# A twelve-stage transformer block on one core: LayerNorm's tiles shared by VectorE and ScalarE, small products in step with its statistics, one barrier per stage, gathers issued further ahead, and the last sums made in the output

## The reference

```
def _layernorm(x, axis=-1, eps=1e-05):
    m = jnp.mean(x, axis=axis, keepdims=True)
    v = jnp.var(x, axis=axis, keepdims=True)
    return (x - m) / jnp.sqrt(v + eps)
...
    x = x + _L0_xattn_ref(_layernorm(x, axis=-1), ctx_768, ...)   # 16 heads of 64 over the context
    x = x + _L0_attn_ref(_layernorm(x, axis=-1), ...)             # 16 heads of 16, relative bias
    x = x + _L0_ffn_ref(_layernorm(x, axis=-1), ...)              # gated, FP4 quantised
    x = x + _L1_xattn_ref(_layernorm(x, axis=-1), ctx_768, ...)
    x = x + _L1_attn_ref(_layernorm(x, axis=-1), ...)             # one head of 256
    x = x + _L1_ffn_ref(_layernorm(x, axis=-1), ...)              # low rank
    x = x + _L2_xattn_ref(_layernorm(x, axis=-1), ctx_768, ...)
    x = x + _L2_attn_ref(_layernorm(x, axis=-1), ...)             # a scan over the 32 tokens
    x = x + _L2_ffn_ref(_layernorm(x, axis=-1), ...)              # 8 experts, top 2, capacity 160
    x = x + _L3_xattn_ref(_layernorm(x, axis=-1), ctx_768, ...)
    x = x + _L3_attn_ref(_layernorm(x, axis=-1), ...)
    x = x + _L3_ffn_ref(_layernorm(x, axis=-1), ...)              # 8 experts, top 2, gelu
    return x
```

## Time and profile before

| what | value |
| --- | --- |
| median of 3 runs | 1863.27 us (1859.93 to 1864.88) |
| the profiled execution, its own time | 1854.92 us |
| its span, first to last instruction | 1852.8 us |
| mean granted TensorE clock | 0.939 of full speed |
| PE busy | 1617.7 us, 87% |
| DVE busy | 1109.5 us, 60% |
| ACT busy, POOL busy | 817.1 us, 792.2 us |

### The profile page before, as it was taken

How to read it: one execution, slowest core, us unless ns; L and a number is a source line. 1 busy time by engine, 2 the same in 40 slices (tenths; PEclk the granted TensorE clock), 3 DMA queues, 4 the chain that set the end, 5 groups by cost and what they waited for, 6 DMA issues and landing times. The chain is left out here.

```text
span 1852.8 us, 35956 instructions
## 1 busy us (share of the span) xinstructions
PE 1617.7 (87%) x12777; PEld 1376.1 (74%) x12777; DVE 1109.5 (60%) x3057; ACT 817.1 (44%) x2383; POOL 792.2 (43%) x934
## 2 busy tenths in 40 slices
PE   6999999766887999987899999969959888859997
PEld 5899989634556999965798889845648745548996
DVE  5888786468854888845666766728951132363331
ACT  4766666213324888831666666620003212113332
POOL 7656656253337999833111111116732420102332
PEclk9999999789897999998999999989969989979998
DMA  8554554200013343302533333251036285761222
GB/s 257 176 169 152 175 164 153 79 1 1 1 28 121 137 139 124 130 18 90 162 107 113 115 106 114 82 187 36 1 103 205 30 210 138 253 218 36 37 40 46
DMA packets 139520, 206.20 MB, mean 111 GB/s; under 512 B 21410, under 2 KB 107106, under 8 KB 138706
## 3 DMA queue, kind: packets, MB, share of 16 engines
q1 hardware_dynamic: 131922, 194.07, 32.8%
q0 software_dynamic: 6720, 8.79, 3.0%
q10 hardware_dynamic: 704, 1.05, 0.2%
HBM read 163.53 MB, written 42.19 MB: 111 GB/s over the span
## 5 line engine op out<-in xcount | busy, mean ns | idle before, releaser
L810 DVE TENSOR_SCALAR xattn_oT<-bank,xattn_last 128x256 f32<-128x256 f32 x256 | 111.8, 478 | 91.7 <-PE bank L631 91.7
L716 ACT ACTIVATE xattn_probs<-bank,xattn_negmax 128x257 f32<-128x257 f32 x256 | 123.7, 483 | 65.5 <-DVE xattn_negmax L791 65.4
L721 ACT ACTIVATE xattn_probs<-xattn_probs,xattn_rsum 128x257 f32<-128x257 f32 x256 | 131.9, 515 | 1.4 <-DVE xattn_rsum L795 1.4
L1036 POOL TENSOR_SCALAR xattn_probs<-xattn_probs,xattn_rsum 128x257 f32<-128x257 f32 x128 | 119.5, 933 | 23.6 <-DVE xattn_rsum L1273 23.5
L791 DVE TENSOR_REDUCE xattn_negmax<-bank 128x1 f32<-128x257 f32 x256 | 106.5, 416 | 34.8 <-PE bank L604 33.2
L800 DVE TENSOR_TENSOR xattn_probsT_lo<-bank,xattn_probsT_hi 128x256 fp32r<-128x256 f32 x256 | 105.1, 410 | 9.8 <-ACT xattn_probsT_hi L727 8.7
L611 PE MATMUL bank<-ident,xattn_probs 128*128 128x128 f32 x512 | 103.9, 285 | 7.0 <-ACT xattn_probs L721 6.5
L147 ACT COPY xnT<-bank 128x512 f32<-128x512 f32 x40 | 21.4, 590 | 200.6 <-PE bank L137 200.6
L727 ACT CAST xattn_probsT_hi<-bank 128x256 fp32r<-128x256 f32 x256 | 95.4, 373 | 32.3 <-PE bank L611 28.2
L549 POOL COPY ctx_stat<-xattn_mv 128x2 f32<-128x2 f32 x32 | 6.0, 188 | 237.9 <-DVE xattn_mv L824 237.9
L600 PE MATMUL bank<-xattn_ctxT,xattn_qk_hi 128*128 128x258 f32 x256 | 93.8, 367 | 0.5 <-DVE xattn_qk L787 0.5
(11 more groups left out here) (488 smaller groups left out, 5332.6 us busy)
## 6 DMA issues: line engine op xcount, KB each, us to landing
xattn_ctxT<-ctx_partsT SPq DMA_DIRECT2D x64, 516.0 KB, 4.0
xattn_ctxN<-ctx_partsN SPq DMA_DIRECT2D x64, 384.0 KB, 4.2
ctx_partsT<-xattn_ctxT SPq DMA_DIRECT2D x32, 516.0 KB, 2.6
moe_w<-in_L_ffn_W SPq DMA_DIRECT2D x16, 1024.0 KB, 12.9
ctx_partsN<-xattn_ctxN SPq DMA_DIRECT2D x32, 384.0 KB, 3.5
moecap_w_early<-in_L_ffn_w SPq DMA_DIRECT2D x10, 1024.0 KB, 9.3
xattn_rawN<-in_ctx SPq DMA_DIRECT2D x32, 192.0 KB, 2.7
xattn_raw<-in_ctx SPq DMA_DIRECT2D x32, 192.0 KB, 4.3
```

What stands on the lines that cost most here:

```text
L716: nc.scalar.activation(probs[:, n % RING, :], SB[n % 2][:, 0:KV], ACT.Exp, bias=negmax[:, n % RING:n % RING + 1], accum_out=psum[:, n % RI ...
L721: nc.scalar.mul(probs[:, n % RING, :], probs[:, n % RING, :], rsum[:, n % RING:n % RING + 1]).then_inc(norm_ready, 1)
L810: nc.vector.tensor_scalar(oT[k][:, heads, b, :], by_head(OB[:, k * 2 * P:(k + 1) * 2 * P]), last[:, k, j * PER_TILE + b:j * PER_TILE + b + ...
L1036: nc.gpsimd.tensor_scalar(probs[:, n % RING, :], probs[:, n % RING, :], rsum[:, n % RING:n % RING + 1], None, ALU.mult).then_inc(norm_read ...
```

## The change

- **One barrier.** `Stage.end` has no barrier of its own. The semaphores of a stage are cleared by POOL once the Block's barrier is passed, while the other engines are already in the next stage, and their numbers are kept from use for one stage (`resting`).
- **Shared LayerNorm.** With `shared=True` the tiles 2, 3, 6 and 7 are normalised by ACT as x times rstd plus shift. DVE computes shift, minus mean times rstd, for two tiles at once. This holds in nine stages (xattn0, attn0, attn1, lowrank, xattn2, scan, moecap, attn3, moe). ACT does its four tiles ahead of its first copy of xnT.
- **Warm products.** `warm` issues two of the bf16 products after each tile's statistics, 16 in all, ahead of the transposes. It stands in xattn0, attn0, xattn2, scan, moecap and moe, where there was nothing, and takes the place of keep_busy in attn1, attn3 and xattn3. lowrank keeps its 34.
- **Gathers.** In moecap XS + 1 experts are gathered ahead, and then each gather goes one expert further.
- **Sums in the output.** moe's table of sums is the output tensor itself, with 128 spare rows that the host cuts off. The eight copies are gone. SP waits for the last additions.

```
@@ Stage.end
-        self.core.nc.clear_and_free_semaphores(self.sems)
-        self.core.nc.all_engine_barrier()
+        core, nc = self.core, self.core.nc
+        nc.clear_and_free_semaphores(self.sems)
+        for rested in core.resting:
+            nc.release_semaphore(rested)
+        core.resting = [nc.alloc_semaphore(f"{self.name}_rests{k}", num=sem.num) for k, sem in enumerate(self.sems)]
@@ Norm
+        self.by_act = [t for t in range(TILES) if shared and t % 4 >= 2]
+        self.by_dve = [t for t in range(TILES) if t not in self.by_act]
...
             dve.wait_ge(self.rstd_ready, h + 1)
+            theirs = [t for t in half if t in self.by_act]
+            if theirs:
+                of = slice(theirs[0], theirs[-1] + 1)
+                nc.vector.scalar_tensor_tensor(self.shift[:, of], self.mv[:, of, 0], -1.0, self.rstd[:, of],
+                                               ALU.mult, ALU.mult).then_inc(self.shift_ready, 1)
             for t in half:
-                nc.vector.tensor_scalar(xn[:, t, :], x[:, t, :], self.mv[:, t, 0:1], self.rstd[:, t:t + 1],
-                                        ALU.subtract, ALU.mult).then_inc(self.xn_ready, 1)
+                if t in self.by_dve:
+                    nc.vector.tensor_scalar(xn[:, t, :], x[:, t, :], self.mv[:, t, 0:1], self.rstd[:, t:t + 1],
+                                            ALU.subtract, ALU.mult).then_inc(self.xn_ready, 1)
...
+    def warm(self, pe, bank):
+
+        for t in range(TILES):
+            pe.wait_ge(self.stats_done, t + 1)
+            self.core.keep_busy(2, bank)
...
+    def act_tiles(self, act):
+        for h, half in enumerate(self.HALVES):
+            act.wait_ge(self.shift_ready, h + 1)
+            for t in half:
+                if t in self.by_act:
+                    self.core.nc.scalar.activation(self.xn[:, t, :], self.core.x[:, t, :], ACT.Identity, bias=self.shift[:, t:t + 1],
+                                                   scale=self.rstd[:, t:t + 1]).then_inc(self.xn_act_ready, 1)
...
     def act(self, act, group=None):
         core = self.core
+        if self.by_act and not group:
+            self.act_tiles(act)
@@ attn1 and attn3; the same line replaces keep_busy(16, 7) in xattn3 and is new in six stages
-            core.keep_busy(20, 7)
+            ln.warm(pe, 7)
             ln.pe(pe)
@@ moecap, POOL
-            for n in range(XS):
+            for n in range(XS + 1):
                 gather(n)
             for n in range(E):
-                if n + XS < E:
-                    gather(n + XS)
+                if n + XS + 1 < E:
+                    gather(n + XS + 1)
                 add(n)
@@ moe
-        self.rows = Rows(core, ctx, "moe", self.E, P)
+        self.rows = Rows(core, ctx, "moe", self.E, P, core.out)
...
-            put_out(sp, range(0, TILES, 2))
-            sp.wait_ge(put, TILES * 16)
+            for z in range(YS):
+                sp.wait_ge(y_added[z], 16 * len(range(z, BLOCKS, YS)))
...
-            put_out(act, range(1, TILES, 2))
```

More of the change, by code:

```diff
@@ L82, with __init__ @@
     HALVES = [range(0, TILES // 2), range(TILES // 2, TILES)]
-    def __init__(self, st, twice=False, xn=None):
+    def __init__(self, st, twice=False, shared=False):
         self.core, self.twice = st.core, twice
-        self.xn = st.core.xn[:, :, :] if xn is None else xn
+        self.xn = st.core.xn[:, :, :]
+        self.by_act = [t for t in range(TILES) if shared and t % 4 >= 2]
+        self.by_dve = [t for t in range(TILES) if t not in self.by_act]
         self.stats = st.sb("ln_stats", [P, TILES, 6])
@@ L90, in __init__ @@
         self.rstd = st.sb("ln_rstd", [P, TILES])
+        self.shift = st.sb("ln_shift", [P, TILES])
         self.stats_done = st.sem("ln_stats_done")
@@ L94, in __init__, with ready, all_ready @@
         self.rstd_ready = st.sem("ln_rstd_ready")
+        self.shift_ready = st.sem("ln_shift_ready")
         self.xn_ready = st.sem("ln_xn_ready")
+        self.xn_act_ready = st.sem("ln_xn_act_ready")
         self.turned = st.sem("ln_turned")
         self.xnT_ready = st.sem("ln_xnT_ready")
+    def ready(self, eng, t):
+        if t in self.by_act:
+            eng.wait_ge(self.xn_act_ready, self.by_act.index(t) + 1)
+        else:
+            eng.wait_ge(self.xn_ready, self.by_dve.index(t) + 1)
+    def all_ready(self, eng, end=TILES):
+        eng.wait_ge(self.xn_ready, len([t for t in self.by_dve if t < end]))
+        if self.by_act:
+            eng.wait_ge(self.xn_act_ready, len([t for t in self.by_act if t < end]))
     def dve(self, dve, meanwhile=None):
@@ L128, in pool @@
             pool.wait_ge(self.veps_done, h + 1)
-            nc.gpsimd.tensor_tensor(self.rstd[:, of], self.veps[:, of], self.core.neghalf[:, of],
-                                    ALU.pow).then_inc(self.rstd_ready, 1)
+            nc.gpsimd.tensor_tensor(self.rstd[:, of], self.veps[:, of], self.core.neghalf[:, of], ALU.pow).then_inc(self.rstd_ready, 1)
+    def warm(self, pe, bank):
+        for t in range(TILES):
+            pe.wait_ge(self.stats_done, t + 1)
+            self.core.keep_busy(2, bank)
     def pe(self, pe, group=None):
@@ L528, in _ @@
             pool.wait_ge(bo_loaded, 16)
-            pool.wait_ge(ln.xn_ready, TILES)
+            ln.all_ready(pool)
             if first:
@@ L2035, in _ @@
             ln.dve(dve)
-            dve.wait_ge(ln.xn_ready, TILES)
+            ln.all_ready(dve)
             for k in range(AHEAD):
@@ L2062, in stage_scan @@
         st = Stage(core, ctx, "scan")
-        ln = Norm(st)
+        ln = Norm(st, shared=True)
         w = st.sb("w", [P, CD, 3 * D])
@@ L2385, in __init__ @@
         self.x = nc.dram_tensor(f"{name}_rows", (TOKENS + spare, D + experts), F32, kind="Internal").ap()
-        self.sum = nc.dram_tensor(f"{name}_sum", (TOKENS + spare, D), F32, kind="Internal").ap()
+        self.sum = sums if sums is not None else nc.dram_tensor(f"{name}_sum", (TOKENS + spare, D), F32, kind="Internal").ap()
         self.cleared = outer.enter_context(nc.semaphore(f"{name}_cleared"))
@@ L2400, in store @@
         for h, half in enumerate(Norm.HALVES):
-            sp.wait_ge(ln.xn_ready, half[-1] + 1)
+            ln.all_ready(sp, half[-1] + 1)
             rows = self.x[half[0] * P:(half[-1] + 1) * P, 0:D]
@@ L2777, in stage_moe @@
         y_added = [st.sem(f"y_added{k}") for k in range(YS)]
-        put = st.sem("put")
         steps = st.sem("dve_steps")
         block = ctx.enter_context(nc.Block())
-        out = core.out.rearrange("b s n -> (b s) n")
         def expert_of(eng, n):
             return eng.value_load(expert_u[0:1, n:n + 1], min_val=0, max_val=E - 1)
-        def put_out(eng, tiles):
-            for z in range(YS):
-                eng.wait_ge(y_added[z], 16 * len(range(z, BLOCKS, YS)))
-            for t in tiles:
-                eng.dma_start(out[t * P:(t + 1) * P, :], rows.sum[t * P:(t + 1) * P, :]).then_inc(put, 16)
         @block.sync
@@ L3236, in project @@
                 mm.then_inc(y_done, 1)
-            core.keep_busy(16, 7)
+            ln.warm(pe, 7)
             ln.pe(pe, 0)
@@ L3506 @@
         dram[name] = nc.dram_tensor(f"in_{name}", a.shape, _mybir.dt.from_np(a.dtype), kind="ExternalInput").ap()
-    out = nc.dram_tensor("out_0_dram", (BATCH, SEQ, D), F32, kind="ExternalOutput").ap()
+    out = nc.dram_tensor("out_0_dram", (TOKENS + P, D), F32, kind="ExternalOutput").ap()
     program(nc, dram, out)
     r = _run(nc, [arrays], core_ids=[0])
-    return r.results[0]["out_0_dram"]
+    return r.results[0]["out_0_dram"][0:TOKENS].reshape(BATCH, SEQ, D)
```

28 lines of the change are left out of this document (15 added, 13 removed).

## The result

The changed kernel takes 1830.2 us, the median of 4 runs (1825.6 to 1832.1), against 1861.8 us before. The ratio is 0.9825, interval 0.9801 to 0.9849. The forecast was 1844, range 1837 to 1852: the sign was right and the size too small. The kernel was measured twice more beside other experiments, each time with before on the same chip: 0.9872 (0.9845 to 0.9900) and 0.9861 (0.9833 to 0.9890). The medians of its three measurements are 1830.2, 1832.0 and 1829.7. Those of before lie at 1856 to 1860 in the later ones, so by medians the effect is 25 to 32 us (24 to 33 by the ratios), and 19 was too little in each of the three. In the experiments, one of the four executions of warm_alone took 5527.6 us and is left out of its median and its ratio.

A forecast was written before the change was run, and what follows sets the result against it. TensorE was busy for 87% of the span, so gains were sought only where it, or everybody, waits. Terms 7.4 + 6.2 + 3.3 + 0.3 + 1.8 = 19.0 us; 1863.3 - 19.0 = 1844.3, range 1837 to 1852.

The forecast's parts named there:

- my -1.8 for the clock: Warm products ahead of the transposes raise TensorE's clock: attn0 -1.3, moecap's gate -1.7, moe's gate +1.2, in all -1.8 us.
- I carry the difference over: The runs' median, 8.35 us above the profiled execution, was kept as the base: 1863.3 - 19.0 = 1844.3.
- -7.4: At the 11 boundaries inside, the second barrier's wait goes, between 6.6 and 8.8 us, taken as 7.4.
- -6.2: At the kernel's end, the output copies go: SyncE leaves at 1845.6 instead of 1851.8, 6.2 us.
- without the copies it leaves when the addition has landed: Step at the end: SyncE leaves moe's Block once the last addition has landed, 1851.8 - 1845.6 = 6.2 us.
- -3.3: In moecap, TensorE's 3.33 us wait for the fifth expert's gather goes, unless that expert's weights are late.
- the -0.3: Shared LayerNorm makes full xnT 0.35 us early at best; counted in attn1 as 0.3, with gates counted separately.
- the half is whole 0.3 sooner: Step in shared LayerNorm: ACT's two tiles take 0.94 us after the shift, so a half ends 0.3 us sooner.
- the heads where a load decides: In xattn0, scan, xattn3 and attn0 first products wait for a load, so a faster LayerNorm gives 0.
- I gave this 5 in 100: Chance 0.05 left for the clock's phase in places the change doesn't touch, to either side, without a size.
- The clock holds: Rival: attn0 and moecap stay at full clock, moe keeps its own; 23.8 us gained, 1839.5; chance 0.2.
- The case against it, that transposes hold the clock down: Rival: moe's gate goes to half clock and loses 3.0; sum 14.2, 1849.1 us; chance 0.05.

The follow-up runs named there:

- warm_alone: Kernel 4: before with only the small products in step with the statistics added; 1850.1 us, 0.9937.
- kernel 9: Before with 72 tiny products ahead of the first stage's transposes, which move TensorE's later code by 144 places; 1847.6 us, 0.9947.
- kernel 2: The changed kernel without the small products, with keep_busy back in attn1, attn3 and xattn3; 1836.1 us, 0.9881.
- kernel 7: Before with only the second barrier taken out (the new Stage.end); 1844.0 us, 0.9936.
- kernel 10: The changed kernel with 56 tiny products ahead of the first stage's own, 256 places with its own 144; 1831.3 us, 0.9850.
- kernel 12: Kernel 6 with three small products per tile of statistics in place of two; 1835.2 us, 0.9869.
- kernel 3: The changed kernel with the second barrier behind each stage again; 1839.9 us, 0.9910.
- kernel 13: Kernel 2 with 72 tiny products in the first stage, LayerNorm still shared; 1831.0 us, 0.9862.
- kernel 14: The changed kernel, unaltered, measured a third time; 1829.7 us, 0.9861.
- kernel 15: Kernel 13 without the sharing, LayerNorm on VectorE alone; 1838.0 us, 0.9899.
- kernel 6: The changed kernel without sharing, all eight tiles of LayerNorm on VectorE; 1826.3 us, 0.9843.
- kernel 11: Kernel 6 measured once more beside other executions; 1826.6 us, 0.9827.

## Why the prediction was wrong

The terms that the traces and runs show are 7.4 for the barrier, 4.4 for the end, 3.3 for the gathers and 3.4 for code that I hadn't counted, 18.5 in all. The change gave 24 to 33 us by the ratios. What is left, 5 to 14 us, stands against my -1.8 for the clock. That is the step that failed: I costed the clock in attn0 and the two gates, and its time at half clock fell in the middle of other stages as well. TensorE's busy time at half clock went from 147 to 110 us by the means of the profiles; at full clock the same work takes half, so by my estimate TensorE was spared some 18 us, not all of it on the path. Term by term:

- **The base.** "I carry the difference over" failed. It took 1863.3, the median of three runs, as what the kernel does. Before's medians in the later jobs are 1856.5 to 1859.7. So against those 4 to 7 of the 14 us by which 1844 missed come from there; in the result's own measurement, with before at 1861.8, it is 1.5. Profile against profile the change gave 1854.9 - 1832.1 = 22.8.
- **Code, a term that I didn't have: -3.4.** attn3's 4.0 less its second barrier's 0.6; kernel 9, with both barriers, gives 3.7. I read TensorE's waits and not their "issue" rows; "PE bank L45 <- issue: 3.8, 1, 3.8" stood among them. The page "Runtime: NRT & Kernel Launch" of the Trainium skill, section "Instruction fetch mechanics", says that an engine's code comes in blocks of 256 instructions over DMA and that this is mostly hidden. The blocks agree: moving the code by 256 places brought the wait back to the very product, the nineteenth, of kernels 2 and 7, and moving it by 144 took it away. Counting all of TensorE's records in each trace from 0 (products, weight loads, and what else stands on its queue) says the same: the first one behind the stop is number 24001 in five of the seven profiles and 24257 in the other two (kernels 10 and 12), 256 further, and none of the 38 products stands at such a place in the other ten. Short waits in attn1, 2.1 us in kernel 12, 0.5 in kernel 3 and 0.4 in kernel 4, are at number 13505, which is 41 times 256 before 24001. "Mostly" hidden agrees too: the queue that carries the packet has 105 of them in the trace of before, which has 27011 such records, 105 times 256 and a rest, and I found one that TensorE stopped for. That one costs 2.7 to 4.2 us in attn3. That the code's packet is late because the weights fill the DMA engines is argued from the share of 99.6%; no run took the weights away.
- **One barrier: the size of -7.4 was right as a wait.** The waits in the trace fell by that much. Kernels 7 and 3 give 12 (7 to 17) and 8 to 10, so some microseconds more than the wait are likely, and aren't shown.
- **The end: -6.2 was -4.4.** The step "without the copies it leaves when the addition has landed" is right of SyncE. What I left out is POOL's drain, 5.83 us long and covered by the copies: the Block's barrier waits for it too.
- **Gathers: -3.3 right.** The weights weren't late, and the idle time is gone.
- **Shared LayerNorm: the -0.3 isn't there.** The step that failed is "the half is whole 0.3 sooner". The last tile of xn is written 6.28 us after attn0's release with the sharing and 6.31 without it: two tiles take ScalarE 1.09 us where I took 0.94, they follow a shift, and so end no sooner than VectorE's four. ScalarE's copies then begin behind its tiles. xnT was 0.3 sooner in attn0, 8.5 to 8.2 from the release, but it isn't the sharing that did it: with small products and VectorE alone it is 7.9, and with the sharing and no small products 8.6. What the sharing costs or gives in the whole, 4 us lost beside the small products and 7 gained without them, is larger than the heads show and of either sign; where it comes from stays open. I also named xattn3 among the heads where a load decides, but nothing is shared there.
- **Small products: -1.8 covered three heads, and the clock changed elsewhere too.** In the heads that I priced it came out about right: VectorE took the first keys of attn0 19.2 and 17.6 us after the release before, and 18.2, 15.6 and 17.8 us now, 1.2 sooner by the means where I took 1.3; moecap's gate gave 2.1, and moe's lost 0 to 2.3. TensorE's busy time at half clock fell from 143 and 151 us in all to 108, 102 and 119, and 9 less in moecap and 6 less in attn3 are part of it in every profile. Part of it lies in falls of the clock in the middle of a stage, as in xattn3, 86 us into it, in the second profile of before:

```profile
1568.00:1573.90 5.90, 4.87 (x41) 2.96 (x40) 1.60 (x5) 2.11 (x5) 0.00 (x0) 1.00 0.00 0
1573.90:1584.10 10.20, 9.17 (x41) 5.02 (x40) 1.02 (x3) 2.15 (x5) 0.00 (x0) 0.50 0.00 1
```

and not in the changed kernel:

```profile
1557.00:1564.00 7.00, 5.28 (x41) 3.10 (x42) 0.43 (x3) 3.45 (x8) 0.00 (x0) 1.00 0.00 0
```

The instructions are the same, and the third profile of the changed kernel has 20 us at half clock in this stage again. So the same instructions come with a fall in some profiles and without it in others, and what decides it wasn't found. I gave this 5 in 100 and no size; in xattn3 alone the means differ by 4.4 us.
- **The chances.** "The clock holds", 1839.5, was the nearest case. The range left out that the clock could change outside the heads. The case against it, that transposes hold the clock down, didn't come: the granted clock was 1.00 over attn0's transposes in the changed kernel, behind the small products.

What stays open: how the clock's part splits between the small products, the shorter boundaries and luck. With the code moved alike, three pairs of kernels price the same products: 0 to 1 us with the sharing (kernels 13 and 14), 11.5 us without it (15 against 6 and 11), and 2 us without it and with both barriers (9 and 4, by the ratios; by the medians kernel 9 is even the faster). It isn't shown that the products as such are worth more than my 1.8. A kernel's time seems to carry some microseconds that nothing measured here explains; that they belong to how its stages happen to lie is a guess.

The best version by its medians is the changed kernel with LayerNorm on VectorE alone: 1826.3 and 1826.6 us in two measurements, 0.9843 (0.9815 to 0.9872) and 0.9827 (0.9803 to 0.9851). Beside it in one job the changed kernel took 5.7 us more.

## What to carry to other kernels

Read an engine's "issue" waits before you call its idle time somebody's fault: inserting instructions anywhere ahead moves where its code is fetched, and an experiment that adds or removes many of them needs a control with the same number placed where they do nothing else. Even that control moved this kernel's time by some 6 us that its one wait doesn't explain, so price a part by more than one pair of kernels before you believe a few microseconds. When a copy or a wait at the end is taken out, look which queue was covered by it; a drain of POOL behind an indirect DMA was. Don't carry the distance of one profile to a median of three runs into a forecast, when the runs of the kernel spread by 1%.

## What the runs showed of the hardware

- TensorE stops for code in the middle of attn3: 2.7 to 4.2 us in seven of the seventeen profiles, none in the other ten, always ahead of the instruction that is number 24001 or 24257 of its trace, at the same product when its code was moved by 256 places, with one 16 KB packet of the kind "instruction" inside the wait, beside a DMA load of 99.6% and more.
- POOL's drain at the end of moe's Block starts 0.2 us ahead of the last accumulating indirect DMA and takes 5.7 to 6.0 us in the seventeen profiles, while that DMA lands 3.6 to 3.8 us after its issue.
- Accumulating DMAs to the output tensor land in 3.5 to 5.3 us in twelve profiles, those to an internal one in 3.6 to 4.7 us in five; the median of the changed kernel is 3.8, as before.
- Normalising 128x256 tiles takes ScalarE 1.09 us for two and VectorE 1.38 us for four (attn0, the changed kernel and before).
